# Four layers of gated cross-attention: scores a second time in rows of keys in the plain attention, two expert mixtures computed in rows, and the key stores of the masked attention moved ahead in the DMA queue

## The reference

```python
for l in range(4):
    x = x + tanh(g_xattn[l]) * attention_l(layernorm(x), ctx)
    x = x + tanh(g_ffn[l]) * ffn_l(layernorm(x))
```

```python
attn = softmax(einsum("bqhd,bkhd->bhqk", q, k) * 8 ** -0.5)   # attention 1
out = einsum("bhqk,bkhd->bqhd", attn, v).reshape(B, 56, 128) @ w_o.T
```

```python
y[t] = sum_e cw[t, e] * (x[t] @ W[e])            # ffn2
y[t] = sum_e cw[t, e] * (x[t] @ W[e] + b[e])     # ffn3
```

## Time and profile before

| | |
|---|---|
| median of 3 runs | 6254.86 us (6254.1 to 6259.9) |
| the profiled execution | 6263.05 us, its span 6261.3 us |
| TensorE multiplications | 5379.5 us busy, 86% |
| TensorE weight loads | 3896.8 us, 62% |
| VectorE | 4432.3 us, 71% |
| ScalarE | 3198.4 us, 51% |
| GpSimd | 1820.4 us, 29% |
| mean granted clock of TensorE | 0.927 |

### The profile page before, as it was taken

One profiled execution on the slowest core, in us unless ns is written; L12 is line 12 of the kernel. 1 busy time (PEld: TensorE's weight loads), 2 busy tenths in 40 slices (PEclk: granted clock), 3 DMA queues, 4 the chain that ended last, 5 costly groups with the idle time before them and its releaser, 6 DMA issues. The chain is left out here.

```text
span 6261.3 us, 134129 instructions
## 1 busy us (share of the span) xinstructions
PE 5379.5 (86%) x51967; PEld 3896.8 (62%) x51967; DVE 4432.3 (71%) x9168; ACT 3198.4 (51%) x5984; POOL 1820.4 (29%) x1426
## 2 busy tenths in 40 slices
PE   2888889899569999989749999999999759999997
PEld 1777777777258888877724444444444437888786
DVE  6888888887257777763458777777777437777774
ACT  0666666666236666652224444444444216666662
POOL 4767676763022222211101111111111012222220
PEclk6899999999679999989969999999999769999998
DMA  4555555553167777742010000000000048888880
GB/s 110 120 125 122 124 123 121 124 119 82 37 123 139 139 140 139 140 87 103 26 33 15 15 15 15 18 17 15 15 15 5 7 94 159 159 161 160 158 151 10
DMA packets 368548, 545.59 MB, mean 87 GB/s; under 512 B 115780, under 2 KB 248006, under 8 KB 367606
## 3 DMA queue, kind: packets, MB, share of 16 engines
q1 hardware_dynamic: 365894, 533.81, 41.7%
q0 software_dynamic: 2048, 3.67, 0.2%
HBM read 413.45 MB, written 123.90 MB: 86 GB/s over the span
## 5 line engine op out<-in xcount | busy, mean ns | idle before, releaser
L652 DVE CUSTOM_DVE_ANT_0 attn_logits<-attn_scores,attn_shift 112x750 f32<-112x750 f32 x1024 | 945.0, 933 | 441.3 <-PE attn_scores L456 441.3
L568 ACT ACTIVATE attn_probs_t<-attn_pt 125x448 f32<-125x448 f32 x1536 | 831.0, 542 | 579.3 <-PE attn_pt L471 559.0
L471 PEld LDWEIGHTS attn_pt<-ident,attn_logits 112*125 112x125 f32 x6144 | 850.9, 188 | 178.6 <-issue 92.5
L471 PE MATMUL attn_pt<-ident,attn_logits 112*125 112x112 f32 x6144 | 920.1, 273 | 25.5 <-ACT attn_logits L559 24.4
L2264 PE MATMUL attn2k_pk<-attn_wk,attn2k_cn_t 128*125 128x512 f32 x1536 | 738.7, 603 | 53.3 <-ACT attn2k_cn_t L2335 36.8
L2275 PE MATMUL attn2k_pg<-attn2k_kn,attn2k_cn 125*128 125x512 f32 x1536 | 725.0, 594 | 6.1 <-ACT attn2k_gram L2343 3.9
L2430 DVE TENSOR_REDUCE attn2k_ss<-attn2k_sq 125x16 f32<-125x1024 f32 x384 | 466.9, 1216 | 256.9 <-ACT attn2k_sq L2372 256.9
L385 POOL CAST attn_k_parts<-xn_t 128x500 bf16<-128x500 f32 x192 | 199.5, 1039 | 1421.6 <-DVE xn_t L622 1421.6
L1159 ACT ACTIVATE attn_probs_t<-attn_pt 125x448 f32<-125x448 f32 x768 | 414.9, 541 | 309.9 <-PE attn_pt L1047 308.2
L2372 ACT ACTIVATE attn2k_sq<-attn2k_pk 125x1024 f32<-125x1024 f32 x384 | 391.9, 1021 | 324.9 <-PE attn2k_pk L2264 324.8
L2264 PEld LDWEIGHTS attn2k_pk<-attn_wk,attn2k_cn_t 128*125 128x125 f32 x1536 | 273.1, 187 | 416.9 <-issue 321.0
(11 more groups left out here) (364 smaller groups left out, 10562.6 us busy)
## 6 DMA issues: line engine op xcount, KB each, us to landing
attn_k_packed<-k_scratch SPq DMA_DIRECT2D x384, 375.0 KB, 6.4
attn_k_packed<-k_scratch SPq DMA_DIRECT2D x384, 187.5 KB, 3.9
k_scratch<-attn_k_parts SPq DMA_DIRECT2D x64, 1125.0 KB, 7.4
attn_ctx_t<-in_ctx_t SPq DMA_DIRECT2D x64, 750.0 KB, 7.3
k_scratch<-attn_k_parts SPq DMA_DIRECT2D x96, 375.0 KB, 4.4
attn_ctx_t<-in_ctx_t SPq DMA_DIRECT2D x96, 250.0 KB, 5.2
attn2k_ctx<-in_ctx SPq DMA_DIRECT2D x32, 750.0 KB
attn_mask_in<-in_mask SPq DMA_DIRECT2D x192, 109.4 KB
```

The lines of the kernel that those rows point to most:

```text
L471: last = pe.transpose(pt[(3 * at + t) % 2][0:KC, (c % 4) * PAIR:(c % 4 + 1) * PAIR], logits[:, at % 3, c * KC:(c + 1) * KC], g.ident[0:PAI ...
L568: act.activation(probs_t[0:KC, p // 4, 4 * t:4 * t + 4, (p % 4) * PAIR:(p % 4 + 1) * PAIR], pt[(3 * at + t) % 2][0:KC, 0:QUAD].rearrange(" ...
L652: dve.tensor_tensor_reduce(out=logits[:, at % 3, cols].rearrange("p (b k) -> p b k", b=2), in0=scores[h][0:PAIR, :, 0:QTR], in1=shift[:, n ...
```

## The change

It has three parts.

1. In the masked attention SP's order at the end of a sequence becomes: key stores of thirds 0 and 1, three key loads, the store of third 2, three key loads, and then the three context loads.
2. Attention 1 gets a function of its own, `direct_attention`. VectorE only takes the maximum of the scores (`top`) and negates it. GpSimd splits the negative maximum into three bf16 parts (`part`), TensorE turns them into three rows (`rows`), and ScalarE puts these as rows 96 to 98 under the queries in `q_blocks` (`place`). Rows 96 to 98 of `k_packed` hold ones. `turn` no longer transposes logits: it makes the scores again, with 125 keys as the stationary and the 112 queries as the moving operand, so that they come out in rows of keys and with the maximum already subtracted. `lower` and the copy of the logits are gone. The next pair's first score waits for the `place` of the pair before the last. Key work on GpSimd moves to pairs 1 to 3, the query blocks to pair 4.
3. `ffn2` and `ffn3` become one function, `mixture`, in one block. The experts' matrices are loaded with the router's. TensorE multiplies a tile of 112 tokens by all 8 experts at once (2 x 512 columns), in rows and without waiting for cw. For 11 tiles VectorE multiplies by cw and sums over the experts; for 5 tiles ScalarE makes 8 products and GpSimd adds them. VectorE adds gate x result to x itself, so the transposes and the update of y in the next `norm` and in `last` fall away (`gate` is None there, as it already was after ffn1). In ffn3 the bias goes by quarters of the tokens.

```diff
@@ norm
                 if out is not None:
-                    sp.wait_ge(x_ready, NQ)
+                    if gate is not None:
+                        sp.wait_ge(x_ready, NQ)
@@ masked_attention, SP
-                    for i in range(3):
-                        if n + 1 < B:
-                            load_keys(n + 1, 1, (2 * i, 2 * i + 1))
-                        if n + 2 < B:
-                            store_keys(n + 2, i)
-                        if n + 3 < B:
+                    if n + 2 < B:
+                        store_keys(n + 2, 0)
+                        store_keys(n + 2, 1)
+                    if n + 1 < B:
+                        load_keys(n + 1, 1, (0, 1, 2))
+                    if n + 2 < B:
+                        store_keys(n + 2, 2)
+                    if n + 1 < B:
+                        load_keys(n + 1, 1, (3, 4, 5))
+                    if n + 3 < B:
+                        for i in range(3):
                             load_ctx(n + 3, i)
@@ direct_attention, GpSimd
+                def part(n, p):
+                    at = n * HP + p
+                    neg, rest = neg_top[:, n % 2, p:p + 1], neg_rest[:, at % 2:at % 2 + 1]
+                    to = neg_parts[:, n % 2, p, :]
+                    pool.wait_ge(neg_ready, at + 1)
+                    pool.tensor_copy(to[:, 0:1], neg).then_inc(neg_split, 1)
+                    pool.wait_ge(neg_split, 4 * at + 1)
+                    pool.tensor_tensor(rest, neg, to[:, 0:1], ALU.subtract).then_inc(neg_split, 1)
+                    pool.wait_ge(neg_split, 4 * at + 2)
+                    pool.tensor_copy(to[:, 1:2], rest).then_inc(neg_split, 1)
+                    pool.wait_ge(neg_split, 4 * at + 3)
+                    pool.tensor_tensor(to[:, 2:3], rest, to[:, 1:2], ALU.subtract).then_inc(neg_split, 1)
...
+                        if 1 <= p < 4 and n + 2 < B:
+                            split(n + 2, p - 1)
+                        if p == 4 and n + 1 < B:
+                            blocks(n + 1)
+                        part(n, p)
@@ direct_attention, TensorE
+                def score(n, p, h):
...
+                    wait(pe, tops_ready, at - 1)
+                    if h == 0:
+                        wait(pe, rows_ready, n * HP + p - 1)
...
+                def rows(n, p):
+                    at = n * HP + p
+                    pe.wait_ge(neg_split, 4 * at + 4)
+                    pe.wait_ge(tops_ready, min(2 * at + 3, 2 * HP * B))
+                    wait(pe, rows_ready, at)
+                    pe.matmul(scores[0][PACKED:FULL, 0, 384:384 + PAIR], neg_parts[:, n % 2, p, :], ident16[:],
+                              start=True, stop=True).then_inc(rows_turned, 1)
+                def turn(n, p, t):
+                    at = n * HP + p
+                    if t == 0:
+                        pe.wait_ge(rows_ready, at + 1)
+                    wait(pe, exp_ready, 3 * at + t - 1)
+                    for c in range(4 * t, 4 * t + 4):
+                        last = pe.matmul(pt[(3 * at + t) % 2][0:KC, (c % 4) * PAIR:(c % 4 + 1) * PAIR],
+                                         k_packed[:, n % 2, p, c * KC:(c + 1) * KC],
+                                         q_blocks[:, n % 2, p, :, :].rearrange("p a s -> p (a s)"),
+                                         start=True, stop=True)
+                    last.then_inc(pt_ready, 1)
...
+                        side_work(n, p)
+                        if n + p > 0:
+                            rows(*(n, p - 1) if p > 0 else (n - 1, HP - 1))
+                        if some:
+                            turn(*before, 2)
@@ direct_attention, ScalarE
+                def place(n, p):
+                    act.wait_ge(rows_turned, n * HP + p + 1)
+                    act.activation(q_blocks[PACKED:FULL, n % 2, p, :, :].rearrange("p a s -> p (a s)"),
+                                   scores[0][PACKED:FULL, 0, 384:384 + PAIR], ACT.Copy).then_inc(rows_ready, 1)
...
+                        for t in range(3):
+                            if t == 2 and last[0] >= 0:
+                                place(*last)
+                            if before[0] >= 0:
+                                exp(*before, t)
+                            if p == 0 and t == 0 and n > 1:
+                                finish(n - 2)
+                            if t == 1 and p < 3 and n + 2 < B:
+                                keep(n + 2, p)
@@ direct_attention, VectorE
+                def top(n, p, h):
+                    dve.wait_ge(scores_ready, 2 * (n * HP + p) + h + 1)
+                    dve.tensor_reduce(tops[:, n % 2, p, h:h + 1], scores[h][0:PAIR, :, 0:QTR], AX.XY,
+                                      ALU.max).then_inc(tops_ready, 1)
...
+                dve.memset(k_packed[PACKED:FULL, :, :, :].rearrange("r j p k -> r (j p k)"), 1.0).then_inc(packed_ones, 1)
@@ mixture (in place of route, experts, ffn2, ffn3), TensorE
+                for t in range(TILES):
+                    if t >= 3:
+                        if t - 3 in ACT_TILES:
+                            pe.wait_ge(parts_ready, ACT_TILES.index(t - 3) + 1)
+                        else:
+                            pe.wait_ge(scaled_ready, DVE_TILES.index(t - 3) + 1)
+                    for c in range(2):
+                        last = pe.matmul(py[t % 3][0:PAIR, c, :], g.xn_t[:, t * PAIR:(t + 1) * PAIR],
+                                         we[:, 4 * c:4 * c + 4, :].rearrange("p e d -> p (e d)"), start=True, stop=True)
+                    last.then_inc(y_ready, 1)
...
+                        wait(pe, x_steps, 2 * q)
...
@@ mixture, ScalarE
+                    for e in range(E):
+                        last = act.activation(parts[:, i % 2, e, :], values(t)[:, e, :], ACT.Copy, scale=cw[:, t, e:e + 1])
@@ mixture, VectorE
+                for i, t in enumerate(DVE_TILES):
+                    dve.wait_ge(y_ready, t + 1)
+                    wait(dve, summed, i - 1)
+                    dve.tensor_tensor(scaled[:, i % 2, :, :], values(t),
+                                      cw[:, t, :].unsqueeze(2).broadcast_to((PAIR, E, D)), ALU.mult).then_inc(scaled_ready, 1)
+                    dve.wait_ge(scaled_ready, i + 1)
+                    dve.tensor_reduce(total[:, t, :], scaled[:, i % 2, :, :].rearrange("p e d -> p d e"), AX.X,
+                                      ALU.add).then_inc(summed, 1)
@@ program
-            gate = n // 2 + 4 * (n % 2) if n != 3 else None
+            gate = n // 2 + 4 * (n % 2) if n not in (3, 5, 7) else None
```

524 lines of the change are left out of this document (416 added, 108 removed).

## The result

The changed kernel takes 6387.53 us (median of 4 runs, 6383.08 to 6394.9) against 6257.38 us before on the same chips: 1.0209 times as long, interval 1.0192 to 1.0227. It is 2.1% slower; 6092 us was forecast, 6030 to 6170 for the range.

The account below looks back on a forecast made before the run. TensorE was taken to lead both attentions, though with gaps; -70 (masked), -20 (plain), -38 (ffn2) and -35 (ffn3) gave -163 us, so 6100 for the profiled execution and 6092 us for the median, range 6030 to 6170.

Parts of the forecast that it names:

- the change list of the plain attention: Plain attention: shorter turns and removed passes against the added maximum chain and the fill; stage -20 us.
- Rival (3): Plain attention: the new chain's gaps halve the clock for share f; slower kernel from f = 0.28 on; chance 0.06.
- The turn: Plain attention: bf16 weight load of 125 columns roughly halves, a group of four takes 0.22 to 0.25 us instead of 0.42.
- rival (1): Plain attention: turns don't get shorter, or the new chain binds in every pair; +15 to +62 us; chance 0.18.
- The walk of a sequence: Plain attention: eight pair lengths worked out to 30.6 us per sequence instead of 31.36, giving -25 us.
- The fill: Plain attention: VectorE fills the ones rows in 21 us, mostly under its 15.94 us idle time; +5 us.
- Masked attention: Earlier key stores end VectorE's wait, shorten TensorE's stall and keep its clock; -70 us, bounds -30 and -90.
- Rival (2): Masked attention keeps its clock dip, or the wait moves to the context load: -50 or -20 us; chance 0.2.
- Mixtures: ffn2 and ffn3: expert values computed in rows ahead of the router's weights; -38 us and -35 us.
- The sum for ffn2's tiles: ffn2: 16 tiles by VectorE (27 us) and TensorE (27.5 less three tiles ahead, plus 2) put at 29.5 us.
- turns that stay at 0.43: Plain attention's bad end: turn groups don't get shorter, 4.4 us of work come back, half previously hidden; +62 in all.
- rival (4): More gain than forecast: plain attention's chain covered, stage -60, or masked attention -90; 6030 to 6060 us; chance 0.12.

Follow-up runs that it names:

- e2: Changed kernel without the plain attention's six key loads from the third sequence on (a probe, scores use old keys); 6216.3 us, against 6262.4 before on the same chip.
- e6: Changed kernel with three buffers of packed keys instead of two, so key loads start earlier, one per head pair; 6295.4 us, against 6290.1 before on the same chip.
- e5: Changed kernel with the old plain attention put back, but its key loads wait as late as in the new one; 6285.6 us, against 6262.4 before.
- e4: Changed kernel with the chain shortened: TensorE issues rows before the side work, ScalarE does place before keep; 6398.1 us, against 6290.1 before on the same chip.
- e7: Changed kernel with both three key buffers and rows and place early; 6204.0 us, against 6290.1 before on the same chip.
- e12: Changed kernel with the old plain attention put back and the wait that paces its key loads removed, so early but dense; 6269.5 us, against 6288.3 before.
- e11: Changed kernel with old plain attention and late key loads, at most two under way, context and store each behind the one before; 6375.1 us, against 6263.7 before.

## Why the prediction was wrong

- **The step that failed** is the change list of the plain attention. It went through the turn, the chain and the fill, and left out a wait that the diff changes too: SP's `pack_keys` no longer waits for scores but for turns before it may fill a key buffer, since the turns now read it. I costed it at nothing without naming it. It moves six loads by two pairs and undoes the spacing of the first four, and that brings 170 us (e2, without the loads; e6, with all of them, started earlier, gives back 134; in the old attention the wait alone costs 133, e5).
- **The mechanism that I did not have** is that data transfers can hold up TensorE's own instructions. Nothing in the rows of before shows it, as no stop occurs there. But the DMA share of 0.70 stood in the earlier trace rows, and I asked for each transfer only whether it would land in time.
- **Rival (3)**, the one for slower at 0.06, had the right symptom, a clock at half in the plain attention, and its f = 0.28, from which the kernel is slower, fits roughly: 480 of 1339 us are at half, f = 0.36. Its cause, gaps of up to 1 us in the new chain, makes some 45 us in e2 without any stop, 37 of them counted in pair 2, which keeps its clock once the chain is shorter (e4, e7). But most of the loss comes from the stops, of which it knows nothing, so that "slower" came true by luck as much as by its reason. Its chance was too small.
- **The turn, right**: a group takes 0.22 us, as the bf16 row said. The first half of rival (1) falls with it, and the second, a chain that binds in every pair, is seen in two pairs of eight only (62 waits for `place`, 34.9 us). By the rule of the Trainium skill, TensorE: Matmul & The Clock Gate, Weight-path perf modes, the load of 125 columns would get no fast load and take an estimated 104 ns. The trace doesn't agree for this form: four pairs of load and multiplication take 0.22 us together.
- **The walk of a sequence**, 30.6 against 31.4 measured: mis-sized by 0.8 us, 26 us in all. Pair 0 takes 4.46 where I had 4.2, although `place` itself takes 257 ns and not 300, so the handoffs around it are slower than the 0.25 I gave them; pairs 2 to 5 take 0.15 more each.
- **The fill**, 20.06 us for 21 worked out, but 13.7 and not 5 us show: I took all of VectorE's idle time before its first operation as cover, and the fill starts 6.87 us into it.
- The late loads, the chain's gaps, the walk and the fill are 170 + 45 + 26 + 9 = 250 us, against the 249 between -20 and +229. The 45 are what e2 leaves once the others are named, so the sum closes by construction.
- **Masked attention**, -40 for -70: the wait for the store went as forecast (50.6 us); the stall was to shrink to 2.4 us and keep the clock, and it did neither (3.05 us, clock to 0.60), as VectorE's test now stands beside GpSimd's addition and takes 1.40 us. Rival (2) names the clock dip and is nearer with its -50; it doesn't name the longer test.
- **Mixtures**, -60 for -73: right in kind. The sum for ffn2's tiles is not what its terms give: 27.5 less three tiles of 1.72 plus 2 is 24.3 for TensorE, below VectorE's 27, and 29.5 was put in; the tiles cost VectorE 11 x (1.22 + 1.92) = 34.5. The strided sum, whose price I bounded at double, is 1.57 times the plain one; the bias's quarters were 1.4 us too cheap each.
- **Slips in the bounds**: 2.2 us x 32 on top of -20 is +50, not +62, for turns that stay at 0.43. In rival (4) a stage of -60 alone gives 6052 and a masked attention of -90 alone 6072, so 6030 to 6060 covers the first and both together, not the second alone.

Still open: what exactly makes an instruction block start late. That it is the number of queued data transfers fits e2, e5, e6 and e12, but the run that was to show it with the same late start (e11) brought new waits. Why pair 2 loses the clock in some sequences and not in others isn't settled either.

## What to carry to other kernels

When a change makes an operand be read later, the wait that frees its buffer moves as well: look for it in the DMA issuer's program, and treat its transfers as moved. A wait that spaces transfers can be worth more than one that protects them; in a program with tens of thousands of short multiplications, look at the idle time that the profile puts down to nothing, and at the instruction queue's packets ahead of it. And price an operation that is freed from a wait by what runs beside it at the new time, not by its old duration.

## What was unexpected in the hardware

- TensorE stopped for 1.2 to 6.1 us in straight code, 27 times in a stage, each stop ending 2.4 to 3.9 us after the start of a 16 KB instruction block and standing, within 3 instructions, where a new block begins, while q1 moved data on all 16 DMA engines (102% in the window shown).
- Six loads of 375 KB issued in 2.7 us instead of 19.5 were enough for it, without any other change, but only in the second half of the stage (e12).
- VectorE's fill costs 0.84 ns per element, of bf16 (20.06 us for 24,000) as of float32 (15.06 us for 18,000).
- The same VectorE test on 125x512 elements takes 0.42 us when it starts 0.15 us ahead of a GpSimd cast, and 1.40 us when a GpSimd addition of two tensors is already under way: it ends 0.28 us behind it. There are 30 places of each.
